# Fixed scratch regions per expert, two batches of 14 token tiles and row-wise loads in a routed expert kernel

## What is computed

```python
scores = sigmoid(x @ gate_w.T)            # 64 experts
# of 8 groups of 8 experts the 4 best (by the sum of their two best scores) stay, then the 8 best experts
rw = weights of the 8 chosen, divided by their sum, times 2.5, else 0
expert_out = vmap(lambda g, u, d: silu(x @ g.T) * (x @ u.T) @ d.T)(Wg, Wu, Wd)   # 88 hidden units each
out = einsum('eth,te->th', expert_out, rw) + shared_mlp(x)
x = layernorm(x + out)
```

## Time and profile before

| | |
|---|---|
| three runs | 694.42, 696.62, 696.30 us; median 696.3 |
| profiled execution | the profile gives its span, 693.7 us from the first to the last instruction; what lies around it is not in the profile |
| busy, share of the span | TensorE 626.5 us (90%), VectorE 465.1 (67%), POOL 446.9 (64%), ScalarE 343.7 (50%) |
| granted TensorE clock | mean 0.979 |
| DMA | 128.5 MB; fills 8 x 2048 KB and 4 x 2560 KB, 104 loads and 104 stores of 256 KB, 224 scatters, 224 gathers |
| chain that ended last | TensorE 74%, VectorE 11%, ScalarE 6%, POOL 4% |

### The profile page before, as it was taken

The page is one execution under the profiler, slowest core; times in us unless marked ns, Lnnn a source line. Parts: engine busy times, 40 slices in busy tenths (PEclk is TensorE's granted clock), DMA queues, the critical chain, the costliest instruction groups (busy, mean ns, idle before and its releaser), DMA issues.

```text
span 693.7 us, 13702 instructions
## 1 busy us (share of the span) xinstructions
PE 626.5 (90%) x3808; PEld 516.4 (74%) x3809; DVE 465.1 (67%) x1287; ACT 343.7 (50%) x673; POOL 446.9 (64%) x463
## 2 busy tenths in 40 slices
PE   3998769888889899999999998999999999999991
PEld 2665546665555589999999998999999976666660
DVE  3468785888546368766776766656365677969684
ACT  8598518663462145455554553555555535422521
POOL 1000017777777777777777777777777777777772
PEclk9999997999999999999999998999999999999996
DMA  8999995111111357777777786888888683312221
GB/s 249 420 418 257 341 414 225 50 50 51 53 54 50 114 179 223 223 224 224 226 231 215 223 220 173 219 233 231 227 230 228 194 266 91 99 49 54 65 68 49
DMA packets 141799, 128.50 MB, mean 185 GB/s; under 512 B 11542, under 2 KB 127086, under 8 KB 141294
## 3 DMA queue, kind: packets, MB, share of 16 engines
q1 hardware_dynamic: 127430, 98.73, 45.7%
q0 software_dynamic: 14336, 29.39, 14.0%
HBM read 56.77 MB, written 71.30 MB: 185 GB/s over the span
## 4 chain that ended last, share of the span: by engine, by line
PE 74%; DVE 11%; ACT 6%; POOL 4%; issue 4%; DMA 1%; POOLq 0%; DVEq 0%; ACTq 0%
PE GU L841 18%; PE OT L861 14%; PE XT L830 7%; PE HT L850 6%; POOL arena L548 4%; PE GU L898 4%; PE GU L899 4%; PE XT L907 4%; PE OT L647 3%; PE GU L626 2%; PE GU L627 2%; PE GU L777 2%; PE GU L778 1%; ACT x1r L979 1%; PE MI L618 1%
## 5 line engine op out<-in xcount | busy, mean ns | idle before, releaser
L540 POOL DMA_INDIRECT xs_dram<-x1r,slots x224 | 225.3, 1006 | 165.8 <-DVE slots L1355 97.8
L548 POOL DMA_INDIRECT arena<-os_dram,slots x224 | 219.4, 980 | 68.3 <-issue 58.5
L841 PE MATMUL GU<-wgu_sb,arena 128*128 x832 | 143.0, 315 | 0.1
L841 PEld LDWEIGHTS GU<-wgu_sb,arena 128*128 128x128 f32 x832 | 125.5, 192 | 0.4 <-issue 0.3
L1471 DVE TENSOR_TENSOR mlpw_sb<-GU,mlpw_sb 128x352 f32<-128x352 f32 x104 | 54.5, 524 | 98.4 <-ACT mlpw_sb L1095 90.1
L861 PE MATMUL OT<-wd_sb,arena 88*128 x832 | 112.6, 279 | 1.3 <-ACT ol L1105 0.9
L1105 ACT ACTIVATE ol<-OT 128x512 f32<-128x512 f32 x104 | 62.1, 597 | 100.1 <-PE OT L861 100.1
L861 PEld LDWEIGHTS OT<-wd_sb,arena 88*128 88x128 f32 x832 | 102.3, 194 | 3.5 <-issue 2.7
L1095 ACT ACTIVATE mlpw_sb<-GU 128x352 f32<-128x352 f32 x104 | 48.2, 463 | 56.5 <-PE GU L841 54.6
L1480 DVE COPY arena<-HT 88x512 f32<-88x512 f32 x104 | 70.4, 677 | 0.0
L1520 DVE SCALAR_TENSOR_TENSOR x_all<-arena,wk,x_all 128x128 f32<-128x128 f32 x224 | 63.2, 343 | 6.8 <-DMA arena<-os_dram,slots 6.8
(11 more groups left out here) (182 smaller groups left out, 863.7 us busy)
## 6 DMA issues: line engine op xcount, KB each, us to landing
arena<-xs_dram SPq DMA_DIRECT2D x104, 256.0 KB
os_dram<-ol SPq DMA_DIRECT2D x104, 256.0 KB, 2.6
xs_dram<-ol SPq DMA_DIRECT2D x8, 2048.0 KB, 25.3
xs_dram<-ol SPq DMA_DIRECT2D x4, 2560.0 KB, 17.6
wgu_sb<-wgu_dram SPq DMA_DIRECT2D x1, 5632.0 KB
xs_dram<-x1r,slots POOLq DMA_INDIRECT x224, 2.2
arena<-os_dram,slots POOLq DMA_INDIRECT x224, 2.6
wd_sb<-wd_dram SPq DMA_DIRECT2D x1, 2816.0 KB
```

The source lines that it names most:

```text
L540: g.indirect_dma_start(out=xs[b], out_offset=bass.IndirectOffsetOnAxis(ap=slots[:, c:c + 1], axis=0), in_=x1r[:, t, :], in_offset=None).th ...
L548: return g.indirect_dma_start(out=gbuf[:, c % 2, i, k, :], out_offset=None, in_=os[batch_of(c)], in_offset=bass.IndirectOffsetOnAxis(ap=sl ...
L841: ins = mm(GU[:, 2 * r + i // 2, (i % 2) * 2 * I:(i % 2 + 1) * 2 * I], xg[:, r, i * P:(i + 1) * P], wgu_sb[:, bass.ds(at[i], 2 * I)], star ...
```

## The change

- Each batch has its own scratch with a fixed region of 2048 rows per expert. A token's row there is the expert's base plus 128 plus its rank, known as soon as its chunk is ranked, so slots are made chunk by chunk in `take_ranks`. Ranks count on through the tiles of a batch. The tiles of an expert end at its last token's row, so the first of them may begin in the 128 rows ahead of the tokens; only those 128 rows per expert are filled with zeros (`fill`, 4 MB per batch).
- Two batches of 14 tiles (3.5 chunks each): 176 expert tiles each, 88 quads in all. `EARLY` is chunk 0, and scatters follow each chunk's slots. Seven chunks give eight sets of tiles for the gathers (0 to 2 and 4 to 6 below in order: 4, 4, 4, 2 tiles of batch 0 and 2, 4, 4, 4 of batch 1).
- The table of a batch gets a third row, the first row of each tile in `xs` (`place_tiles`, `weight_columns`). SP reads four of them into registers and issues four DMAs of 64 KB per quad.
- The outputs `os` stay packed, so the gathers use other slots (`gather_slots`, once per batch in the shared part).
- The quads of a batch drain before those of the next start; SP issues the next batch's loads behind the last store. Shared chunks 6 and 7 move behind the quads, with buffers that alias the output tiles `ol`.
- `keep_pace` goes. A scatter waits until the one eight before it has landed, a gather round until the round two before it has landed.
- Sums of sets 0 and 1 stand beside quads 60 to 67 and 80 to 87, all others in the dense part.

```diff
-BATCHES = (3, 2, 2)
+TILES = (14, 14)
+STRIDE = 2048
+EARLY = 0
+LAG = 8
+SH_A = 6
+SUM_AT = {0: 60, 1: 80}
+SUMS_IN_DENSE = {2: (0, 1, 8), 3: (8, 2, 8), 4: (12, 2, 8), 5: (18, 1, 8), 6: (34, 1, 8)}
...
+            def fill(b):
+                n = P * P // (K * P)
+                sp.dma_start(xs[b].rearrange("(e r) d -> e (r d)", r=STRIDE)[:, 0:P * P].rearrange("e (n c) -> e n c", n=n),
+                             flat(ol[0:E, 0:2, :]).unsqueeze(1).to_broadcast([E, n, K * P])).then_inc(d_fill[b], 16)
...
             def load(b, q, u):
-                sp.dma_start(xl[:, u % 4, :].rearrange("p (t d) -> p t d", d=P),
-                             xs_t[b][:, bass.ds(q * QUAD, QUAD), :]).then_inc(d_ld[u % 4], 16)
+                rows = nc.values_load_multi_w_load_instructions(
+                    woff[0:1, 2, bass.ds(q * QUAD, QUAD)], engines=[mybir.EngineType.SP],
...
+                for i in range(QUAD):
+                    sp.dma_start(xl[:, u % 4, i * P:(i + 1) * P], xs[b][bass.ds(rows[i], P), :]).then_inc(d_ld[u % 4], 16)
...
             for b in range(NBAT):
+                sp.wait_ge(s_woff, b + 1)
+                sp.wait_ge(d_fill[b], 16)
+                for i in range(LAG):
+                    sp.wait_ge(d_scat[i], 16 * K * TFIRST[b + 1] // LAG)
...
+                for q in range(hi - 7, hi):
+                    store(b, q, q)
...
-                        if (c + 1) % EVERY == 0:
-                            keep_pace(c + 1)
+            for t in range(NST):
+                b = batch_of(t)
+                if t % CT == 0:
+                    pool.wait_ge(s_x1r, t // CT + 1)
+                    pool.wait_ge(s_slot, t // CT + 1)
+                for k in range(K):
+                    n = t * K + k
+                    if n >= LAG:
+                        pool.wait_ge(d_scat[n % LAG], 16 * (n // LAG))
+                    g.indirect_dma_start(
+                        out=xs[b], out_offset=bass.IndirectOffsetOnAxis(ap=slots[:, t * K + k:t * K + k + 1], axis=0),
+                        in_=x1r[:, t, :], in_offset=None).then_inc(d_scat[n % LAG], 16)
...
+            for g_, ts in enumerate(SETS):
+                b = batch_of(ts[0])
+                if ts[0] == TFIRST[b]:
+                    pool.wait_ge(s_gslot, b + 1)
                     for r in range(4):
                         pool.wait_ge(d_st[r], 4 * Q0[b + 1])
                 for k in range(K):
+                    if g_ >= 2:
+
+                        pool.wait_ge(s_acc, ROWS0[g_ - 2] + len(SETS[g_ - 2]) * (k + 1))
+                    if k >= 2:
+                        pool.wait_ge(d_gat[g_ % 2][k - 2], landed(g_))
+                    elif g_:
+                        pool.wait_ge(d_gat[(g_ - 1) % 2][K - 2 + k], landed(g_ - 1))
...
+            pe.wait_ge(s_res, SH_A)
+            pe.wait_ge(s_expw, 32)
+            first_quads(0)
+            last_quads(0)
+            first_quads(1)
+            transpose_weights()
+            last_quads(1)
+            shared_from(SH_A, NC)
...
+            for r in range(4):
+                act.wait_ge(d_st[r], 4 * NQ)
+            for c in range(SH_A, NC):
+                for j in range(SJ):
+                    shared_silu(c, j)
...
             def take_ranks(c):
 
                 dve.wait_ge(p_rank, c + 1)
...
+                v.tensor_tensor(flat(key[:, span(c), :]), HT[:, 0:CT * E], flat(sel[:, ring(c), :]),
+                                ALU.mult).then_inc(s_key, 1)
+                dve.wait_ge(s_key, c + 1)
+                for t in tiles(c):
+                    ins = v.max(keys[:, t, :], key[:, t, :])
+                then(ins)
+                v.tensor_scalar(slots[:, c * CT * K:(c + 1) * CT * K], flat(keys[:, span(c), :]), float(P - 1), None,
+                                ALU.add).then_inc(s_slot, 1)
...
+            def gather_slots(b):
+
+                lo, hi = TFIRST[b], TFIRST[b + 1]
+                dve.wait_ge(s_ended, b + 1)
+                then(v.tensor_tensor(key[:, lo:hi, :], key[:, lo:hi, :], bc(delta[:, b, :].unsqueeze(1), P, hi - lo, E),
                                      ALU.add))
                 for t in range(lo, hi):
                     ins = v.max(keys[:, t, :], key[:, t, :])
                 then(ins)
...
+            weighed(0, 3 * UN, 2 * TILES[0], 6)
+            normalize_weights(0)
+            plain(0, 2 * TILES[0], Q0[1] - UN)
...
+            for k in range(K):
+                quad(1, SUM_AT[0] + k, k)
+                add_round(0, k)
+            weighed(1, SUM_AT[0] + K, SUM_AT[0] + K + 2 * (TILES[1] - mid), TFIRST[1] + mid)
+            normalize_weights(1)
+            plain(1, SUM_AT[0] + K + 2 * (TILES[1] - mid), SUM_AT[1])
+            for k in range(K):
+                quad(1, SUM_AT[1] + k, k)
+                add_round(1, k)
```

More of the change, by code:

```diff
@@ L60 @@
 NOWHERE = -2e38
-FAR = float(1 << 20)
-BATCHES = (3, 2, 2)
[L64 to L68, removed]
+TILES = (14, 14)
+NBAT = len(TILES)
+TFIRST = [sum(TILES[:b]) for b in range(NBAT + 1)]
+NST = TFIRST[-1]
+NS = NST // CT
+CLAST = [(t - 1) // CT for t in TFIRST[1:]]
+STRIDE = 2048
+EARLY = 0
+ROUTED = NS - 1
+ET = [n * K + E for n in TILES]
 ET0 = [sum(ET[:b]) for b in range(NBAT + 1)]
@@ L96 @@
[L96 to L138, removed]
@@ L141, in due, with batch_of @@
-def due(n):
-    done = [s for s in progress() if s[0] <= POOL_AT + STEP * n - SLACK]
-    return done[-1][1:]
+LAG = 8
+assert all(n * P + P <= STRIDE for n in TILES) and all(n % QUAD == 0 for n in ET) and P == 2 * E and NJ == HI
+def batch_of(t):
+    return max(b for b in range(NBAT) if TFIRST[b] <= t)
+SETS = [ts for c in range(NS) for b in range(NBAT)
+        if (ts := [t for t in range(c * CT, (c + 1) * CT) if batch_of(t) == b])]
+NSET = len(SETS)
+ROWS0 = [K * sum(len(ts) for ts in SETS[:g]) for g in range(NSET + 1)]
@@ L147, with landed, added @@
+def landed(g):
+    return 16 * sum(len(SETS[f]) for f in range(g % 2, g + 1, 2))
+def added(c):
+    return ROWS0[max(g for g in range(NSET) if SETS[g][0] // CT == c) + 1]
+SUM_AT = {0: 60, 1: 80}
+SUMS_IN_DENSE = {2: (0, 1, 8), 3: (8, 2, 8), 4: (12, 2, 8), 5: (18, 1, 8), 6: (34, 1, 8)}
+STATS_IN_DENSE = {0: 0, 1: 1, 9: 2, 17: 3, 27: 4, 42: 5}
+ROOT_AT = (11, 29)
+ROOTS = ((0, 3), (3, 5), (5, 6), (6, NC))
 V_NORM, V_CW, V_CB, V_A, V_B, V_MN, V_BG, V_BU = 0, 1, 4, 5, 6, 7, 8, 8 + NM
@@ new lines, in _ @@
+                sp.wait_ge(d_fill[b], 16)
+                for i in range(LAG):
+                    sp.wait_ge(d_scat[i], 16 * K * TFIRST[b + 1] // LAG)
+                lo, hi = Q0[b], Q0[b + 1]
+                for q in range(lo, lo + 4):
+                    if q >= 4:
+                        sp.wait_ge(p_tx, q - 3)
+                    load(b, q, q)
+                for q in range(lo, lo + 4):
+                    load_next(b, q + 4, q)
+                    if q >= lo + 3:
+                        store(b, q - 3, q - 3)
@@ new lines, in ranks @@
+                mm(HT[:, 0:CT * E], ones_bf[:, :], base_bf[:, :].unsqueeze(1).to_broadcast([P, CT, E]),
+                   start=True, stop=False, skip_group_check=True)
+                for b in range(NBAT):
+                    own = [t for t in tiles(c) if batch_of(t) == b]
+                    for s in range(TFIRST[b], own[-1] if own else 0):
+                        lo = max(s + 1, own[0]) - c * CT
+                        n = own[-1] - c * CT + 1 - lo
+                        mm(HT[:, lo * E:(lo + n) * E], ones_bf[:, :],
+                           sel[:, s % (4 * CT), :].unsqueeze(1).to_broadcast([P, n, E]), start=False, stop=False,
+                           skip_group_check=True)
@@ L746, in step @@
                     ranks(c)
-                    starts(0)
                     for m in range(NM // 2, NM):
@@ L1123, in _ @@
             nc.scalar.preload_act_table(ACT.Silu)
-            for c in range(NC):
+            for b in range(NBAT):
+                act.wait_ge(d_fill[b], 16)
+            for c in range(SH_A):
                 for j in range(SJ):
```

529 lines of the change are left out of this document (242 added, 287 removed).

## The result

The changed kernel takes 726.3 us (median of four runs, 724.46 to 729.36) beside 696.0 for the kernel before on the same chip: ratio 1.044, 95% interval 1.041 to 1.047. Slower, as forecast, and inside the range. Timed again later, beside some of the experiments, it gave a median of 721.4 (six runs, 720.62 to 728.76). That is under the 724 to 729 expected of it. The ten together have a median of 723.5 and spread over 8.7 us. The kernel before, timed beside every group of experiments, kept its median within 695.4 to 696.0, so times of different groups are compared directly. The experiments are read against 723.5; a difference under 3 us, or one that a second timing does not repeat, is called none.

The account below looks back on a forecast made before the run. The prediction saw POOL's indirect DMAs and TensorE both full to the end, and expected SP's row loads to set the changed quads' rate. Its path summed to 717.0 us, plus 2.6 from profile to median: 720, range 690 to 750.

Parts of the forecast that it names:

- batch 0, to its last product: Quads of batch 0: three SP units of 2.9 us, 37 of 3.45, landing 2.6, drain 8.9; ends at 375.9.
- boundary and batch 1: Batch 1's loads wait behind batch 0's last store; 161.2 us, plus 1 for normalising; last quad at 538.1.
- dense part's start to set 4's first gather: POOL waits for set 2's first sum, 5.3 us into the dense part, then a handover of 0.9.
- to the last gather: POOL's end: set 4 in step with the sums, 23.0 us, then 96 gathers at 1.284; last starts at 704.2.
- Row loads: SP's loop: register load, four loads and a store take 3.45 us per quad, 0.49 over TensorE's; chance 0.63.
- the other end: Rival in SP's loop: loads stay hidden, quads keep 2.96 us, time 690 to 698 us; chance 0.25.
- POOL's stops: POOL idles twice, before the first gather and before set 4's, the second released by VectorE's sums in the dense part.
- Start of the quads: Ahead of the quads: shared chunks moved -12.7 us, transposition wait +1.1, front end -4.0; first quad from 243.0 to 227.4.
- Landing waits: POOL's scatters: waiting for landings costs nothing while one lands within eight issues, 10 us; it takes 2.2, at most 5.6.
- SP does not keep up: Answers the rival that SP's unit stays within 2.96 us, giving 690 to 698 us; chance 0.25.
- Register loads are not slow: Answers the rival that SP's 0.77 us spacing partly holds, a unit takes 3.8 and the time is 749; chance 0.07.
- Scatters are not slow: Answers the rival that regions 1 MiB apart slow POOL's scatters; at 1.6 us each the time is 762; chance 0.05.

## Why the prediction came out as it did

Its sum and what the profile shows, term by term (us):

| Term | predicted | measured |
|---|---|---|
| first quad | 227.4 | 237.8 |
| batch 0, to its last product | 148.5 | 150.2 |
| boundary and batch 1 | 162.2 | 159.0 |
| shared chunks 6 and 7, to the dense part | 14.9 | 15.4 |
| dense part's start to set 4's first gather | 6.2 | 7.5 |
| to the last gather | 145.0 | 143.1 |
| tail | 12.8 | 13.1 |
| span | 717.0 | 726.0 |

**Row loads, right.** The term that was to decide did: 3.45 us per unit were forecast, 3.49 came once the rows loaded ahead were used up, and the step from row load to row load was 0.52 for 0.56. Leaving three of the four loads out gives the quads their 3.0 us back. The sentence of the Trainium skill that spoke for the other end ("DMA: Bandwidth & Descriptors", section "Issuing engines are not separate DMA queues": issue time is usually small beside the transfer) is not contradicted by one issue, 0.33 us here beside 2.5 to a store's landing. It does not say what five issues in a row cost a quad of 2.96.

**POOL's stops, right where it counted.** Stops before the first gather and before set 4 were forecast, the second with VectorE's sums in the dense part as releaser, and both came. The second was sized by the same sum: gathers from 559.2, came 569.85, later by what the start of the quads was off. A third, 11.7 us before set 3, was not forecast: batch 0's gathers were to be done at some 524, and the last of them started at 548.15. It cost nothing, since set 4 waited for set 2's sums until 569.85 anyway.

**Start of the quads, wrong.** The step put the front end at -4.0 and the first quad at 227.4. Chunk 7's rows came 4.8 us later than before instead (195.31; 190.49 in the kernel before), 8.8 off. ScalarE's timeline of the normalised rows gives the parts:

```profile
39.28 1.65 ACT L946 ACTIVATE x1r<-arena,nmean,inv 128x128 f32<-128x128 f32 x4 [0.44 <-DVE nmean L1203]
...
71.11 1.65 ACT L946 ACTIVATE x1r<-arena,nmean,inv 128x128 f32<-128x128 f32 x4 [0.44 <-DVE nmean L1203]
...
130.69 1.65 ACT L946 ACTIVATE x1r<-arena,nmean,inv 128x128 f32<-128x128 f32 x4 [1.34 <-DVE nmean L1203]
...
157.29 1.65 ACT L946 ACTIVATE x1r<-arena,nmean,inv 128x128 f32<-128x128 f32 x4 [2.13 <-DVE nmean L1203]
```

The step with the early routing takes 31.8 us (39.28 to 71.11) where it took 33.0 at chunk 2 (78.46 to 111.42): 1.2 saved, 3.2 were forecast. The step that places batch 0's tiles takes 26.6 (130.69 to 157.29) where the step that assigned batch 1's slots took 22.9: 3.7 lost, where 1.3 were to be saved net (2.8 less 1.5, and the 1.5 came from no row). That is the largest miss, 5.0. The other steps lost 2 together, 0.5 were forecast. The remaining 1.6 of the 10.4 at the first quad were lost in the shared part. In other profiles with the same front end the placing step took 24.9 to 26.8 us and the first quad came at 234.0 to 237.8, so some 4 us of the miss change from one execution to the next.

**Landing waits, wrong, and hidden behind the first miss.** "The landing waits cost POOL nothing" held for most of the span: POOL waited for ten landings in 224. It failed from the tenth scatter on, for some 22 us (POOL's timeline):

```profile
74.78 0.96 POOL L495 DMA_INDIRECT xs_dram<-x1r,slots  x1 [1.67 <-DMA xs_dram<-x1r,slots]
79.54 1.09 POOL L495 DMA_INDIRECT xs_dram<-x1r,slots  x1 [3.81 <-DMA xs_dram<-x1r,slots]
...
89.50 0.96 POOL L495 DMA_INDIRECT xs_dram<-x1r,slots  x1 [4.17 <-DMA xs_dram<-x1r,slots]
```

The first scatter was right (58 forecast, 58.9), the last of batch 0 not: 220.0 for 205. "In time for 227" then was no more than just so, with row loads from 223.0. The kernel with the later routing, whose scatters also start 10.8 us later, shows the other side: with the front end out of the way the scatters hold the first row load, and the end stays where it is. The step took its 2.2 to 5.6 us from scatters that start at 100.8, behind the experts' weights; starting at 58.9 they ran beside them. The fills, costed at nothing, had landed by then.

**The rivals.** SP does not keep up. Register loads are not slow: 0.30 at the median, though up to 0.9 at worst. Scatters are not slow for the regions' pitch: 1.26 us apart when nothing waits, and neither the time nor the fills changed with another pitch. The Trainium skill's rule on rows a large power of two apart (same page, section "Latency and other measured facts"), for which a chance of 0.05 was kept, does not show in these runs, for scatters or fills.

**The time.** In the first profile the span is 9.0 over the sum, 10.4 of it from the start of the quads; the other terms together are 1.3 under, most by luck of signs, since batch 1 came 3.2 quicker than forecast and four of the others slower. In the second, with the first quad at 234.0, it is 718.9, only 1.9 over. The median of all ten executions is 3.5 above the 720 forecast. The mechanism was right; the term that was mis-sized is the start of the quads.

## What to carry to other kernels

Splitting one transfer into several with addresses from registers is paid on the issuing queue: add up register load, every issue with its spacing and what else stands on that queue, and compare with the time of one turn of the loop it feeds. If the sum is just over, moving one store to a queue with room may be enough. When work is taken out of a stage, ask what the stage behind it waits for next. Here fewer quads only left POOL waiting for sums that had stayed late, and moving those sums was worth as much as mending the queue. A start that has two causes shows no gain from mending one.

## What the runs showed of the hardware that was not expected

- While the fills and then the experts' weights move (40 to 70 us) the DMA engines are busy all the time at 300 GB/s. Beside the weights (to some 92 us) scatters of 64 KB, which land in 2.4 us at the median, took up to 22.7 where sixteen could be in flight; beside fills, in the kernel before, at most 5.6. Two fills of 4 MB from 64 partitions landed 23.5 and 43.8 us behind their issue, and 23.4 and 43.4 with another pitch of their targets.
- In the changed kernel's first profile TensorE comes out of a stretch with pauses at 1.2 GHz: four transposes take 1.1 us at the start of either batch and 0.60 later. When it falls and rises differs between executions of one kernel: in the second profile batch 0 starts at 0.66. The changed kernel, at a mean granted clock of 0.936 where the kernel before has 0.979, spreads over 8.7 us in ten runs; the kernel before stays within 3.5 in all of its own.
- A register load of four values takes 0.30 us on SP in the median and up to 0.9.
